# A two-layer transformer kernel: a gate ahead of ten maxima, the last output tile in halves, and the order of the first loads

## The chip, the cores and the metric

The kernel runs on one core of one Trainium2 chip. The metric is device time in microseconds (us) of one execution, as the median of several runs. The core has a matrix engine (PE, TensorE), VectorE (DVE), ScalarE (ACT), GpSimd (POOL) and SyncE (SP), which only issues transfers. Each engine works through a queue of its own in order; they meet at semaphores. Matrix products land in eight banks of PSUM of 128 partitions by 512 numbers.

## The reference

Two layers on x of shape (2, 512, 512), that is eight tiles of 128 rows, four to a batch b:

```python
xn = _layernorm(x)
x = x + attention0(xn)  # 32 heads of 16, 8 key-value heads, rope, causal softmax
      + ffn0(xn)        # 512 -> 1792 -> 512, silu gate, weights w * (su @ sv)
xn = _layernorm(x)
x = x + attention1(xn)  # 4 heads of 128, sigmoid of the scores, causal
      + ffn1(xn)        # 512 -> 1376 -> 512, silu gate, weights w + 2 * b @ a
```

## The kernel before, in words

All is 32-bit. A product of two 32-bit matrices is made of three faster ones: each operand is split into a high part (a rounded copy) and a low part (the difference), and `three_pass` (lines 50 to 54) issues high x high, low x high and high x low. So nearly every operand has a "hi" made by ACT and a "lo" made by a subtraction on POOL or DVE.

**Front (`qkv_stage`, lines 446 to 755).** SP loads the first four tiles of x (L497), then the key columns of the qkv weights (L498, 128 of 768 columns), then the rest of them (L500, four transfers), the other four tiles (L501) and tables. For each tile DVE takes mean and variance (L88, L90), ACT the root (L94), DVE the reciprocal (L98 or L636). Tiles 0 and 2 are normalised by DVE (L100), tiles 1 and 3 by ACT (L577), which needs a shift from DVE (L640). PE transposes the tile (L108), ACT makes the high part (L117) and DVE the low part (L122). POOL splits the key columns (L538 and L540), ACT and POOL the rest (L593 and L543; the last quarter by DVE, L658). Between the transpositions PE multiplies an identity with itself into a bank that nobody reads (L726), 2, 2, 3 and 5 times; before them it does the same with a tile of ones (L730). The products of keys and queries (`pair`, L706) then start, first `pair(0)`, the keys of batch 0, which waits for all four low parts and for POOL's split of the key columns.

**Attention and up (`attention_stage`, lines 850 to 1217).** The gate and up products of layer 0's feed-forward network and its attention are woven together by steps. There are 14 chunks `o` of 128 hidden columns, each of 16 steps `r` (step = 16 o + r): steps 0 to 3 are the gate of batch 0, 4 to 7 its up, 8 to 11 the gate of batch 1, 12 to 15 its up. A step is one three-pass product of 512 columns. ACT takes tanh of the gate (L277) at steps 4 and 12; DVE forms the gated value (L284, `dve_gate`) at r = 5 and 13 and the hidden value (L290) at r = 8 and at r = 0 of the next chunk. The product of chunk `o` on a bank waits until that bank's last value was read: `pe.wait_ge(self.u if k == 0 else self.h, 2 * o + b)` (line 804), `u` being counted by the gate and `h` by the hidden value.

Every third step, from step 6 on, ends with a burst of attention work. A group is four heads of one batch. In four bursts PE makes scores only to find each row's maximum (L1149, 11 pieces), which DVE reduces (L1095, 16 maxima, each followed by an accumulator read) in two halves; DVE negates each half (L1104), PE transposes the negated values (`minus_max`, L1156), ACT copies them into a row (L1028) and sends two row transfers to the stack of queries (L1038). The final scores (`key_scores`, L1167) need those rows. For group 0 the burst at step 6 has six maxima and the one at step 12 has ten, with both negations; the burst at step 15 has the transposition of the first-finished half, the one at step 18 that of the other. At step 13 POOL makes a low part of the network's factors (L141, `stack_lo`), 32x768, wanted by PE at step 18. SP loads the stack of a later group once the row of the current one has landed (L941, L942). Banks go round in two rings, `wide` and `narrow`, three banks each.

**End (`down1_stage`, lines 1909 to 1956).** The last down projection: for each batch, 11 chunks, each with four tiles' three-pass products over 512 columns (`pe_chunk`, line 385) into four banks that stay open over the chunks. ACT makes the high part of a hidden chunk (L377), POOL the low part (L382). When a tile's last chunk is done, DVE adds the bank to the running sum (L1949) and SP stores 256 KB (L1925).

The lines that are touched most:

```python
def dve_gate(self, dve, o, b):
    dve.wait_ge(self.tanh, 2 * o + b + 1)
    ...
if r in (5, 13):                      # attention_stage, vector, L1124
    up.dve_gate(dve, o, r // 8)
...
for t in range(NT):                   # down1_stage, vector, L1947
    dve.wait_ge(down.full, t + 1)
    dve.tensor_tensor(e.acc[:, t, :], e.acc[:, t, :], down.acc(t)[:, :], ALU.add).then_inc(out_s, 1)
```

## Time and profile before

| | us |
|---|---|
| median of three runs (661.47 to 661.97) | 661.49 |
| the profiled execution, its own time | 659.51 |
| its span, first to last instruction | 657.8 |
| PE busy | 647.8 (98%) |
| DVE busy | 413.1 (63%) |
| ACT busy | 287.9 (44%) |
| POOL busy | 244.4 (37%) |
| granted PE clock, mean | 0.999 |

The profile is one execution. Times in it count from the start of the span. Busy time of PE includes pipelining: a record of 0.39 us for a product of 512 columns overlaps its neighbours, and what counts is the distance between starts. "Idle before" names the work whose semaphore came last. A line number can be that of a helper.

### The profile page before, as it was taken

The page shows a single profiled execution, that of the slowest core. Times are in us where ns is not written, and L with a number is a line of the kernel's source. Part 1 is how long each engine was busy: PE and PEld are TensorE (multiplying, and loading weights), DVE is VectorE, ACT ScalarE, POOL GpSimd, SP SyncE. Part 2 cuts the span into 40 slices and gives each one's busy share as a digit, 9 for nine tenths or more (in the row PEclk, how much of TensorE's full clock was granted, in tenths as well). Part 3 has the DMA queues.
Part 4 walks back from the last instruction along what each step waited for, and adds up shares of the span by engine and source line. Part 5 has one row for each costly group of instructions (what it writes and reads, how often), then busy time and mean ns, then how long its engine had stood idle before and what let it go on. Part 6 is the DMA issues. An engine that isn't in the chain of part 4 may idle for free.

```text
span 657.8 us, 9974 instructions
## 1 busy us (share of the span) xinstructions
PE 647.8 (98%) x3472; PEld 495.5 (75%) x3472; DVE 413.1 (63%) x985; ACT 287.9 (44%) x559; POOL 244.4 (37%) x245
## 2 busy tenths in 40 slices
PE   7999999999999999999999999999999999999998
PEld 6887666666666666666788888888888888888886
DVE  6958777667777677663477665386665655646501
ACT  5333455455455555544344344264444444443321
POOL 4597333123323233323144538503234323323443
PEclk9999999999999999999999999999999999999999
DMA  9457323253323222021255600501011101012011
GB/s 303 138 158 183 96 80 111 80 134 95 90 57 90 79 79 80 18 81 50 74 184 163 211 21 17 147 1 33 32 33 35 62 33 33 32 34 79 15 50 65
DMA packets 23929, 55.17 MB, mean 84 GB/s; under 512 B 3876, under 2 KB 4872, under 8 KB 22824
## 3 DMA queue, kind: packets, MB, share of 16 engines
q1 hardware_dynamic: 23224, 54.35, 27.8%
q8 instruction: 28, 0.46, 0.3%
q10 hardware_dynamic: 656, 0.20, 0.1%
q14 instruction: 21, 0.17, 0.1%
HBM read 42.86 MB, written 11.54 MB: 83 GB/s over the span
## 4 chain that ended last, share of the span: by engine, by line
PE 97%; DVE 2%; DMA 0%; ACT 0%; issue 0%
PE bank L52 26%; PE bank L54 25%; PE bank L53 25%; PE bank L1149 7%; PE bank L1180 6%; PE bank L1167 2%; PE bank L180 2%; PE bank L108 1%; PE bank L1156 1%; PE bank L344 1%; PE bank L1744 1%; DMA x<-in_x 0%; DVE bank L1095 0%; DVE acc L1949 0%; PE bank L1505 0%; DVE minus_max L1104 0%
## 5 line engine op out<-in xcount | busy, mean ns | idle before, releaser
L1095 DVE CUSTOM_DVE_ANT_0 bank<-bank,mask 128x512 f32<-128x512 f32 (+3 forms) x256 | 118.1, 521 | 44.2 <-PE bank L1149 44.0
L217 POOL TENSOR_TENSOR up_w_lo<-up_w_eff,up_w_hi 128x512 fp32r<-128x512 f32 x50 | 66.9, 1346 | 103.0 <-ACT up_w_hi L213 103.0
L382 POOL TENSOR_TENSOR down_h_lo<-hidden,down_h_hi 128x512 fp32r<-128x512 f32 x50 | 65.1, 1304 | 89.0 <-ACT down_h_hi L377 89.0
L52 PE MATMUL bank<-x0T_hi,up_w_hi 128*128 128x512 f32 x224 | 94.7, 423 | 2.6 <-DVE up_gated L284 2.6
L1047 ACT ACTIVATE probs<-bank 128x512 f32<-128x512 f32 x160 | 84.5, 597 | 22.4 <-PE bank L1167 22.4
L54 PE MATMUL bank<-x0T_lo,up_w_hi 128*128 128x512 f32 x224 | 88.5, 395 | 0.0
L53 PE MATMUL bank<-x0T_hi,up_w_lo 128*128 128x512 f32 x224 | 88.4, 395 | 0.0
L52 PE MATMUL bank<-down_w_hi,down_h_hi 128*128 128x512 f32 x200 | 78.3, 391 | 0.0
L53 PE MATMUL bank<-down_w_hi,down_h_lo 128*128 128x512 f32 x200 | 78.0, 390 | 0.0
L999 POOL TENSOR_SCALAR_AFFINE_SELECT probs<-probs 128x512 f32<-128x512 f32 x64 | 39.9, 636 | 98.9 <-ACT probs L1047 98.9
L377 ACT ACTIVATE down_h_hi<-hidden 128x512 fp32r<-128x512 f32 x50 | 31.5, 631 | 89.6 <-PE bank L54 89.6
L284 DVE SCALAR_TENSOR_TENSOR up_gated<-up_tanh,bank 128x512 f32<-128x512 f32 x50 | 34.3, 685 | 42.3 <-ACT up_tanh L277 42.0
L52 PEld LDWEIGHTS bank<-x0T_hi,up_w_hi 128*128 128x128 f32 x224 | 42.1, 188 | 20.1 <-issue 14.1
L1149 PE MATMUL bank<-k_stack,q_stack 48*128 48x512 f32 (+3 forms) x256 | 56.9, 342 | 0.0
L1167 PE MATMUL bank<-q_stack,k_stack 49*128 49x512 f32 x160 | 54.0, 434 | 0.0
L213 ACT ACTIVATE up_w_hi<-up_w_eff 128x512 fp32r<-128x512 f32 x50 | 31.1, 630 | 51.2 <-DVE up_w_eff L204 51.2
L290 DVE SCALAR_TENSOR_TENSOR hidden<-up_gated,bank 128x512 f32<-128x512 f32 x50 | 34.2, 685 | 29.6 <-PE bank L54 29.3
L1149 PEld LDWEIGHTS bank<-k_stack,q_stack 48*128 48x128 f32 x256 | 35.9, 185 | 22.1 <-issue 17.1
L277 ACT ACTIVATE up_tanh<-bank 128x512 f32<-128x512 f32 x50 | 29.7, 594 | 46.5 <-PE bank L54 25.3
L54 PEld LDWEIGHTS bank<-x0T_lo,up_w_hi 128*128 128x128 f32 x224 | 42.1, 188 | 10.2
L53 PEld LDWEIGHTS bank<-x0T_hi,up_w_lo 128*128 128x128 f32 x224 | 42.3, 189 | 6.0
L1708 POOL TENSOR_SCALAR_AFFINE_SELECT weights_T<-weights_T 128x128 f32<-128x128 f32 x32 | 9.9, 310 | 93.5 <-ACT weights_T L1700 93.5
(173 smaller groups left out, 1387.8 us busy)
## 6 DMA issues: line engine op xcount, KB each, us to landing
w_raw<-in_w_gate_up SPq DMA_DIRECT2D x25, 512.0 KB, 3.5
w_raw<-in_w_down SPq DMA_DIRECT2D x25, 256.0 KB, 2.9
q_stack<-q_hi SPq DMA_DIRECT2D x32, 128.0 KB, 3.4
att<-att_T SPq DMA_DIRECT2D x16, 256.0 KB, 2.0
q_hi<-rope_hi SPq DMA_DIRECT2D x8, 256.0 KB
q_lo<-rope_lo SPq DMA_DIRECT2D x8, 256.0 KB
q_stack<-q_lo SPq DMA_DIRECT2D x16, 128.0 KB, 3.4
attention_or_xn<-att SPq DMA_DIRECT2D x16, 128.0 KB
```

The lines of the kernel that those rows point to most:

```text
L52: pe.matmul(out, w_hi, m_hi, start=first, stop=False, skip_group_check=True)
L53: pe.matmul(out, w_lo, m_hi, start=False, stop=False, skip_group_check=True)
L54: return pe.matmul(out, w_hi, m_lo, start=False, stop=last, skip_group_check=True)
L217: pool.tensor_tensor(self.half(self.w_lo[:, o % 2], k), self.half(self.w_eff, k), f32(self.half(self.w_hi[:, o % 2], k)), ALU.subtract).th ...
L284: dve.scalar_tensor_tensor(out=self.ut[:, b, :], in0=self.th[:, b, :], scalar=1.0, in1=self.product_bank(o, b, 0)[:, :], op0=ALU.add, op1= ...
L382: pool.tensor_tensor(self.h_lo[:, k % 2, :], self.hid[:, o, b * S:(b + 1) * S], f32(self.h_hi[:, k % 2, :]), ALU.subtract).then_inc(self.h ...
L999: pool.affine_select(out=diag, in_=diag, compare_op=ALU.is_ge, fill=0.0, base=0, pattern=[[0, REP], [1, P]], channel_multiplier=-1).then_i ...
L1047: act.activation(pt[:, BLOCK_OF[KEY_PIECES[p]], :, :], key_ring(g, p).bank(("keys", g, p))[:, :].rearrange("p (h s) -> p h s", h=REP), ACT ...
L1095: dve.tensor_tensor_reduce(out=own, in0=own, in1=e.mask[:, S - w:S], scale=1.0, scalar=NEG, op0=ALU.add, op1=ALU.max, accum_out=rmax[:, i ...
L1149: last = pe.matmul(bank[:, n * w:(n + 1) * w], qst[K, slot, h + n, i * P:(i + 1) * P], kst[K, slot, 0:w], start=(n == 0), stop=(n == nh - ...
L1167: pe.matmul(key_ring(g, p).bank(("keys", g, p))[:, :], kst[K, slot, j * P:(j + 1) * P], qst[K, slot, :, i * P:(i + 1) * P], start=True, st ...
L1180: last = pe.matmul(bank[32 * h:32 * (h + 1), j * P:], e.v[:, b, j, kv, :], pt[:, own, h, :], start=(j == 0), stop=(j == NJ - 1), skip_grou ...
```

## The change

Three parts. In the front, the key columns are loaded after the third tile of x and before the fourth; DVE normalises tile 3 itself, so that ACT normalises tile 1 only; the identity products become 4, 0, 0 and 9; and POOL begins the low parts of the other weight columns only after the four low parts of x. In the attention stage the gate of chunk 0, batch 1, goes ahead of the burst at step 12 (it stood at step 13); the first transposition of negated maxima follows step 14 instead of step 15; POOL's low part at step 13 waits for the first negation. At the end, the last low part is made by DVE instead of POOL; the last tile's chunks 0 to 8 are added early; its chunks 9 and 10 are left until the other three tiles are done, and are computed, added and stored in two halves of 256 columns in banks 3 and 4, the second half stored from ACT's queue.

```diff
@@ qkv_stage
-        shift = sb("norm_shift", [P, NJ])
+        shift = sb("norm_shift", [P, 1])
-        norm.normed_in_order = {0: (norm.normed, 1), 1: (act_normed, 1), 2: (norm.normed, 2), 3: (act_normed, 2),
-                                **{t: (norm.normed, t - 1) for t in range(NJ, NT)}}
+        norm.normed_in_order = {0: (norm.normed, 1), 1: (act_normed, 1), **{t: (norm.normed, t) for t in range(2, NT)}}
-        IDENTITY_PRODUCTS = (2, 2, 3, 5)
+        IDENTITY_PRODUCTS = (4, 0, 0, 9)
@@ qkv_stage, sync
             for t in range(NJ):
                 sp.dma_start(x_sb[:, t, :], d["x"][t * P:(t + 1) * P, :]).then_inc(x_loaded[t], 16)
-            sp.dma_start(w_raw[:, :, 0:P], d["w_qkv"][:, 0:P].rearrange("(c p) n -> p c n", p=P)).then_inc(w_loaded[0], 16)
+                if t == 2:
+                    sp.dma_start(w_raw[:, :, 0:P], d["w_qkv"][:, 0:P].rearrange("(c p) n -> p c n", p=P)).then_inc(w_loaded[0], 16)
@@ qkv_stage, gpsimd
+            pool.wait_ge(norm.lo, NJ)
             for c in range(NC - 1):
                 pool.wait_ge(w_hi_ready, c + 1)
@@ qkv_stage, scalar
             norm.act_hi(act, 1)
-            normalise(3)
             norm.act_hi(act, 2)
@@ qkv_stage, vector
             norm.dve_norm(dve, 2)
-            reciprocal(3)
-            shift_of(3)
+            norm.dve_norm(dve, 3)
@@ attention_stage
+FIRST_ROW_AT, EARLY_GATE_AT = 14, 12
@@ attention_stage, gpsimd
                     pool.wait_ge(*stage.last_pair_low)
+                    pool.wait_ge(neg_done, 1)
                     stack_lo(pool, e.lr0, e.lr0_raw, slice(0, 0), LR0_REST[part], e.lr0_hi, part + 2, e.lr0_lo)
@@ attention_stage, vector
-                if r in (5, 13):
+                if r in (5, 13) and step != EARLY_GATE_AT + 1:
                     up.dve_gate(dve, o, r // 8)
+                if step == EARLY_GATE_AT:
+                    up.dve_gate(dve, 0, 1)
@@ attention_stage, tensor
                     for half, g in ((0, s["low"]), (1, s["high"])):
-                        if g is not None:
+                        if g is not None and (g, half) != (0, 1):
                             minus_max(g, half)
+                if step == FIRST_ROW_AT:
+                    minus_max(0, 1)
@@ down1_stage
+        LAST = 2 * CH1 - 1
+        HALVES, last_banks = [slice(0, D // 2), slice(D // 2, D)], [e.bank[3], e.bank[4]]
+
+        def store_half(engine, half):
+            t, cols = NT - 1, HALVES[half]
+            engine.wait_ge(out_s, NT + half)
+            engine.dma_start(out[t * P:(t + 1) * P, cols], e.acc[:, t, cols]).then_inc(stored, 16)
...
-            for t in range(NT):
+            for t in range(NT - 1):
                 sp.wait_ge(out_s, t + 1)
                 sp.dma_start(out[t * P:(t + 1) * P, :], e.acc[:, t, :]).then_inc(stored, 16)
-            sp.wait_ge(stored, 16 * NT)
+            store_half(sp, 0)
+            sp.wait_ge(stored, 16 * (NT + 1))
@@ down1_stage, gpsimd
-                for o in range(2 if b == 0 else 0, CH1):
+                for o in range(2 if b == 0 else 0, CH1 - b):
@@ down1_stage, scalar
                 down.act_hhi(act, 1, o)
+            store_half(act, 1)
@@ down1_stage, vector
+            for t in range(NJ):
+                add(t)
+            dve.wait_ge(down.hlo, 2 * CH1 - 1)
+            dve.wait_ge(down.hhi, 2 * CH1)
+            dve.tensor_tensor(down.h_lo[:, LAST % 2, :], down.hid[:, CH1 - 1, S:], f32(down.h_hi[:, LAST % 2, :]),
+                              ALU.subtract).then_inc(down.hlo, 1)
+            t = NT - 1
+            dve.wait_ge(down.mm, 2 * CH1 - 3)
+            dve.tensor_tensor(e.acc[:, t, :], e.acc[:, t, :], down.acc(t)[:, :], ALU.add).then_inc(rest_added, 1)
+            for t in range(NJ, NT - 1):
+                add(t)
+            t = NT - 1
+            dve.wait_ge(rest_added, 1)
+            for half, cols in enumerate(HALVES):
+                dve.wait_ge(down.full, NT + half)
+                dve.tensor_tensor(e.acc[:, t, cols], e.acc[:, t, cols], last_banks[half][:, cols], ALU.add).then_inc(out_s, 1)
@@ down1_stage, tensor
-            for b in range(B):
-                for o in range(CH1):
-                    down.pe_chunk(pe, b, o)
+            for o in range(CH1):
+                down.pe_chunk(pe, 0, o)
+            for o in range(CH1 - 3):
+                down.pe_chunk(pe, 1, o)
...
+            pe.wait_ge(down.hlo, 2 * CH1 - 2)
+            for i in range(NJ):
+                last = product(CH1 - 3, i)
+            last.then_inc(down.mm, 1)
+            pe.wait_ge(down.hlo, 2 * CH1 - 1)
+            for i in range(NJ - 1):
+                product(CH1 - 2, i)
+            pe.wait_ge(down.hlo, 2 * CH1)
+            for i in range(NJ - 1):
+                product(CH1 - 1, i).then_inc(down.full, 1)
+            pe.wait_ge(out_s, 2)
+            for half in range(2):
+                last_product(half, CH1 - 2)
+                last_product(half, CH1 - 1).then_inc(down.full, 1)
```

`product(o, i)` is the three-pass product of chunk `o` for tile `4 + i` over 512 columns; `last_product(half, o)` is that of the last tile over the 256 columns of one half, into bank 3 or 4.

## Rows read from the trace of the kernel before

**Rows 1.** The page, part 4: the chain that ended last, shares by engine.
```profile
PE 97%; DVE 2%; DMA 0%; ACT 0%; issue 0%
```
**Rows 2.** Time line, PE, 63 to 68 (start us, us, engine, line, operation, count, idle before).
```profile
63.70 0.40 PE L52 MATMUL bank<-x0T_hi,up_w_hi 128*128 128x512 f32 x1
...
64.40 0.27 PE L1156 MATMUL bank<-ident,minus_max 128*8 128x128 f32 x1
67.31 0.47 PE L52 MATMUL bank<-x0T_hi,up_w_hi 128*128 128x512 f32 x1 [2.65 <-DVE up_gated L284]
```
**Rows 3.** Time line, 60 to 68, the other engines.
```profile
60.20 0.60 ACT L277 ACTIVATE up_tanh<-bank 128x512 f32<-128x512 f32 x1 [3.03 <-PE bank L54]
...
61.26 0.56 DVE L1095 CUSTOM_DVE_ANT_0 bank<-bank,mask 128x384 f32<-128x384 f32 x1 [1.53 <-PE bank L1149]
...
61.99 1.82 POOL L141 TENSOR_TENSOR lr<-lr_raw,lr 32x768 fp32r<-32x768 f32 x1
...
62.44 1.41 DVE L1104 TENSOR_SCALAR minus_max<-row_max 128x8 f32<-128x8 f32 x1
...
65.00 1.81 ACTq L1038 DMA_DIRECT2D q_stack<-minus_max_rows  x2
...
66.41 0.17 DVE L1104 TENSOR_SCALAR minus_max<-row_max 128x8 f32<-128x8 f32 x1
...
67.27 0.69 DVE L290 SCALAR_TENSOR_TENSOR hidden<-up_gated,bank 128x512 f32<-128x512 f32 x1
...
67.86 0.31 SPq L941 DMA_DIRECT2D q_stack<-q_hi  x1
```
**Rows 4.** Time line, 7 to 13, the front.
```profile
7.33 0.68 DVE L88 BATCH_NORM_STATS2 norm_stats<-x 128x6 f32<-128x512 f32 x1
...
8.31 0.55 DVE L100 TENSOR_SCALAR x<-x,norm_mv,norm_rstd 128x512 f32<-128x512 f32 x1
...
8.53 1.47 POOL L540 TENSOR_TENSOR wqkv_lo<-wqkv_raw,wqkv_hi 128x512 fp32r<-128x512 f32 x1
...
8.55 0.65 PE L108 MATMUL bank<-ident,x 128*128 128x128 f32 x4 [1.03 <-ACT x L577]
...
9.10 1.47 DVE L122 TENSOR_TENSOR x0T_lo<-bank,x0T_hi 128x512 fp32r<-128x512 f32 x2
...
11.08 1.28 PE L726 MATMUL bank<-ident 128*128 128x128 f32 x10
...
12.66 0.50 PE L52 MATMUL bank<-x0T_hi,wqkv_hi 128*128 128x512 f32 x1 [0.29 <-DVE x0T_lo L122]
```
**Rows 5.** Time line, 649 to 656, DVE and POOL.
```profile
649.93 1.29 POOL L382 TENSOR_TENSOR down_h_lo<-hidden,down_h_hi 128x512 fp32r<-128x512 f32 x1 [1.43 <-ACT down_h_hi L377]
...
652.56 2.73 DVE L1949 TENSOR_TENSOR acc<-acc,bank 128x512 f32<-128x512 f32 x4 [27.19 <-PE bank L54]
```
**Rows 6.** Issue of the key weights; transfers issued 2.4 to 2.9, KB, us to landing.
```profile
2.66 0.43 SPq L498 DMA_DIRECT2D wqkv_raw<-in_w_qkv  x1
...
x<-in_x SPq DMA_DIRECT2D x1, 256.0 KB, 4.7
wqkv_raw<-in_w_qkv SPq DMA_DIRECT2D x1, 256.0 KB, 5.1
```
**Rows 7.** Line L100, layer 1's normalisations: ns min/median/max, first and last start.
```profile
L100 DVE TENSOR_SCALAR attention_or_xn<-acc,norm_mv,norm_rstd x8: 545/546/1331, 389.7 to 433.5; 128x512 f32<-128x512 f32 x8
```
**Rows 8.** Time line, PE, 459 to 460: three products of 256 columns, then 512.
```profile
459.62 0.28 PE L52 MATMUL bank<-x1T_first,xk_hi 128*128 128x256 f32 x1
...
459.97 0.40 PE L52 MATMUL bank<-x1T_second,up_w_hi 128*128 128x512 f32 x1
```
**Rows 9.** Line L366, a subtraction of DVE in SBUF: ns min/median/max.
```profile
L366 DVE TENSOR_TENSOR down_w_lo<-down_w_eff,down_w_hi x14: 627/693/1361, 317.4 to 359.7; 128x512 fp32r<-128x512 f32 x14
```
**Rows 10.** The transfer issued between 655.2 and 655.5: KB, us to landing.
```profile
out<-acc SPq DMA_DIRECT2D x1, 256.0 KB, 2.0
```
**Rows 11.** Time line, PE, the first instructions.
```profile
1.81 3.61 PE L730 MATMUL bank<-v_ones 128*128 128x128 f32 x18 [1.81 <-POOL v_ones L536]
```

More of the change, by code:

```diff
@@ L575, in normalise @@
             def normalise(t):
-                act.wait_ge(shifted, 1 + t // 2)
-                act.activation(x_sb[:, t, :], x_sb[:, t, :], ACT.Identity, bias=shift[:, t:t + 1],
+                act.wait_ge(shifted, 1)
+                act.activation(x_sb[:, t, :], x_sb[:, t, :], ACT.Identity, bias=shift[:, :],
                                scale=norm.rstd[:, t:t + 1]).then_inc(act_normed, 1)
@@ L639, in shift_of @@
                 dve.wait_ge(norm.rst, t + 1)
-                dve.tensor_scalar(shift[:, t:t + 1], norm.mv[:, t, 0:1], norm.rstd[:, t:t + 1], -1.0,
+                dve.tensor_scalar(shift[:, :], norm.mv[:, t, 0:1], norm.rstd[:, t:t + 1], -1.0,
                                   ALU.mult, ALU.mult).then_inc(shifted, 1)
@@ L1917, in down1_stage @@
         layer1.up.down_factor_read = [(down.eff, 1), (down.eff, 2)]
-        out_s, stored = sem("out_ready"), sem("stored")
+        out_s, stored, rest_added = sem("out_ready"), sem("stored"), sem("last_tile_rest_added")
+        LAST = 2 * CH1 - 1
[4 more added lines that the diff above has]
+            engine.dma_start(out[t * P:(t + 1) * P, cols], e.acc[:, t, cols]).then_inc(stored, 16)
         def sync(sp):
@@ L1946, in vector, with add @@
             dve.wait_ge(*before["added"])
-            for t in range(NT):
+            def add(t):
                 dve.wait_ge(down.full, t + 1)
                 dve.tensor_tensor(e.acc[:, t, :], e.acc[:, t, :], down.acc(t)[:, :], ALU.add).then_inc(out_s, 1)
-        def tensor(pe):
-            for b in range(B):
-                for o in range(CH1):
-                    down.pe_chunk(pe, b, o)
+            for t in range(NJ):
+                add(t)
+            dve.wait_ge(down.hlo, 2 * CH1 - 1)
@@ new lines, in vector, with product, last_product @@
+            dve.wait_ge(rest_added, 1)
+            for half, cols in enumerate(HALVES):
+                dve.wait_ge(down.full, NT + half)
+                dve.tensor_tensor(e.acc[:, t, cols], e.acc[:, t, cols], last_banks[half][:, cols], ALU.add).then_inc(out_s, 1)
+        def tensor(pe):
+            for o in range(CH1):
+                down.pe_chunk(pe, 0, o)
+            for o in range(CH1 - 3):
+                down.pe_chunk(pe, 1, o)
+            def product(o, i):
+                k, own = CH1 + o, slice(i * P, (i + 1) * P)
+                return three_pass(pe, down.acc(NJ + i)[:, :], down.h_hi[:, k % 2, own], down.h_lo[:, k % 2, own],
+                                  down.high[o], down.low[o], False, o == (CH1 - 3 if i == NJ - 1 else CH1 - 1))
+            def last_product(half, o):
+                k, own, cols = CH1 + o, slice((NJ - 1) * P, S), HALVES[half]
+                return three_pass(pe, last_banks[half][:, cols], down.h_hi[:, k % 2, own], down.h_lo[:, k % 2, own],
+                                  down.high[o][:, cols], down.low[o][:, cols], o == CH1 - 2, o == CH1 - 1)
+            pe.wait_ge(down.hlo, 2 * CH1 - 2)
[12 more added lines that the diff above has]
+                last_product(half, CH1 - 1).then_inc(down.full, 1)
```

## The prediction, made before the result was known

> **What bounds the kernel now.** The page's chain comes first: TensorE (PE) carries 97% of it [rows 1]. So an edit counts only if it shortens PE's instruction stream, a hole in it, or one of its two ends. The time line of PE in the attention stage shows the one long hole inside: the products of step 15 begin at 63.70, the transposition of the negated maxima starts at 64.40, and the first product of step 16 waits until 67.31, 2.65 us idle, put down to the gate on VectorE (DVE) [rows 2]. The other engines' time line says why the gate is late: tanh is ready at 60.80 (60.20 + 0.60), but DVE runs ten maxima and two negations from 61.26 on, and only then the gate, which is done where the hidden row starts, near 67.2 [rows 3]. One negation of 128x8 took 1.41 us and its twin 0.17: the long one ended with the POOL subtraction L141 beside it (61.99 + 1.82 = 63.81) [rows 3]. Next the front: PE starts the key products at 12.66, after the fourth low part on DVE [rows 4]. Last the end: four additions 652.56 to 655.29, then the last store [rows 5].
>
> The sum is made against the profiled execution: span 657.8, its own time 659.51. The median of the three runs shown is 661.49, 1.98 above; I carry the same difference over to it.
>
> **Middle: the gate ahead of ten maxima.** The gate moves from step 13 to step 12 in DVE's queue. It waits for tanh at 60.80, runs 0.69 and ends near 61.52; DVE was idle until 61.26, so the maxima behind it start about 0.3 later. POOL's subtraction now waits for the first negation, so the 1.41 should become 0.17: 1.24 back. Maxima and both negations end near 66.58 (66.41 + 0.17) + 0.3 - 1.24 = 65.6, the hidden row at 66.4 instead of 67.96 [rows 3].
>
> What is PE's next wait? Step 16 needs the gate (61.5) and the low weights of chunk 1, long done; PE arrives at 64.66 and goes on. The new POOL wait holds L141 back to about 62.9 to 64.7; behind it stand only POOL's low weights, wanted only after step 18's factors, and PE's own wait for it at step 18, near 66.1. The moved transposition follows step 14 at 63.70 and finds its negation ready at 62.9. ScalarE copies the row near 64.0 instead of 64.71, and its two row transfers start 0.7 earlier. They took the ACT queue from 65.00 to 66.81, and SP, which waits for the second landing, went on at 67.86; both move to 67.16 at the latest [rows 3]. The first key scores, in step 18's burst, need the first of those rows and come at about 67.2 (64.66 + three steps of 0.70, as from 63.70 to 64.40, + some 0.4 for two factors and the first scores, from 0.23 for 512 columns): in time, by little [rows 2]. The hidden row of 66.4 is wanted at step 20, near 68.7. SP gains no DMA here and its stack loads go 0.7 earlier. The scores at step 12 issue as before; DVE has already given their banks back. So all 2.65 should go. Bounds: 0 to 2.65; I take 2.65, since each successor found has slack. If this cover were gone, the most that could return is the same 2.65.
>
> **Front.** The key weights are issued before the fourth tile of x. Their landings were 2.66 + 5.1 = 7.8, and 2.2 + 4.7 = 6.9 for the tile, whose issue stands about 0.45 before theirs [rows 6]. Swapped, the tile lands between 6.9 and 7.8 (nearest row: the keys, which held that place); I take 7.8. Its statistics were started by DVE at 7.33 and now start near 7.8: +0.45. Normalisation 2 followed them by 0.98 (7.33 to 8.31), so it runs from 8.8 to 9.3. In DVE's queue the small shift of tile 3 goes and a full normalisation of 0.55 comes, with its reciprocal: 9.4 to 9.95. The four low parts took from 9.10 to about 12.6, though two of them are 1.47, so some 0.6 of that was waiting; now they run one after another: 9.95 + 2 x 1.47 = 12.9 at most, 12.7 at 0.69 each [rows 4]. ScalarE loses its normalisation of tile 3, which isn't on this chain any longer. PE: after the fourth transposition, about 10.05 to 10.65, nine identity products instead of five. Ten instructions took 1.28, so a product (two instructions) is about 0.224 and nine are 2.0: end 12.65, the same moment. The key products therefore start near 12.7 against 12.66: 0.0 within a tenth. If the tile still lands at 6.9, both chains are 0.4 shorter: -0.35. If it lands 0.35 later than I say, +0.35. The four products after the first transposition (from about 7.1, 0.9 us) end near 8.0, and PE waits for ScalarE's normalisation of tile 1 until 8.55, so they are free; if that cover were gone, the two added ones would cost 0.45.
>
> A DVE operation that works on SBUF alone can stand still while POOL works: a normalisation took 1.33 us instead of 0.55 once [rows 7]. POOL's key subtraction (1.47, from 8.53, 0.7 after its weights landed) now starts near 7.6 and is over near 9.1; at worst it ends under normalisation 2, which would have ended at 9.3 anyway. POOL's rest of the weights now waits for the fourth low part, 12.7, when ScalarE has just made their first high part anyway; the second pair of products wants it three microseconds later. The queue of SP holds the same transfers with only this swap, so all behind it land as before.
>
> **End.** PE issues the same columns, but twelve products of 256 columns instead of six of 512. Three of 256 take 0.35 (459.62 to 459.97) [rows 8], so twelve take 1.40; three of 512 take 0.68, the pitch at which the four additions follow them (2.73), so six took 1.36: +0.04 at most, within the rounding. The last chunk now starts 0.68 earlier, after three tiles of the chunk before, at about 651.2. POOL's low part would be ready at 651.22 (649.93 + 1.29) [rows 5]; the change gives it to DVE, whose like took 0.63 to 0.69, and 1.36 beside POOL [rows 9]. POOL is done by then, so it is ready near 650.6; even 1.36 would cost only 0.1. The early addition for the last tile (0.69) and this subtraction lie in DVE's idle time ahead of 652.5. After PE's end there remains one addition of 256 columns instead of 0.69. It isn't in the trace; from 512 columns in 0.69 with some 0.15 fixed I estimate 0.42: -0.27. Then the last store: 256 KB landed 2.0 us after its issue [rows 10]. The four stores were issued 0.68 apart, so 256 KB go out in 0.68 or less, 128 KB in 0.34: a half store can be from 0 to 0.34 shorter, and up to 0.4 if it also stood behind its forerunners, which now start 0.7 earlier. The ACT queue issues it while SP is busy. I take 0.18 for the landing, midway: total -0.27 - 0.18 = -0.45, bounds -0.2 and -0.7.
>
> The Trainium skill, page "DMA: Bandwidth & Descriptors", section "Anatomy of one DMA", says that about 2 us of a DMA are fixed, whatever its size, mostly the receipt. By that rule halving the store saves nothing on its landing, and the end brings 0.25 instead of 0.45. The trace gives 2.0 us for 256 KB and has no store of 128 KB from here, so it leaves this open.
>
> **Sum:** -2.65 - 0.45 + 0.0 = -3.1. Profiled execution 656.4 (span 654.7), median 661.49 - 3.1 = 658.4. Bounds: front -0.35 and end -0.7 give 657.8; front +0.35, end -0.2 and a middle that loses 0.6 to a late row give 659.6.
>
> **Rivals.** (A) The front becomes the longer chain. The tile lands 0.4 later still, and POOL's key subtraction starts just ahead of a normalisation and holds it (1.33 instead of 0.55 [rows 7], +0.8): together with what stands above about +1.3, time 659.7. For it: the four low parts have no gap left on DVE. Against it: the key weights come earlier, which takes POOL out of the way.
>
> (B) The other side, slower than before: TensorE drops to its lower level, 1.2 GHz, ahead of the key products, since the identity products between the transpositions go from 2 and 3 to none. The very first products (18 instructions in 3.61, 0.20 each) are nearly twice as far apart as the identity products later (0.112) [rows 4, 11], though the page's clock line shows nothing below nine tenths. A product of 512 columns takes 0.23 at the upper level and would take 0.23 more at the lower; 14 of them eat the whole gain of 3.1, and twenty make 661.49 - 3.1 + 4.6 = 663.0. Against it: PE stood idle for 1.03 us before 8.55 [rows 4] and ran on at the full pace; after the change its gaps are shorter, and it is busy for 2 us right ahead of the key products.
>
> (C) The change doesn't do what it says: step 16 waits for several things, and if another than the gate held it until 67.31, only the end gains: 661.0. Against it: PE's first product starts 0.1 after the gate's end, and the low weights it also waits for stand in POOL's queue ahead of L141, which had started at 61.99 [rows 3].
>
> **How the numbers follow.** Forecast 0.80; A 0.08, 659.7; B 0.06, 663.0; C 0.06, 661.0. What a measurement of this kernel can tell from no change is about 0.2%, 1.3 us: the forecast and A are faster (0.88), C is the same (0.06), B slower (0.06). Range 657.4 to 660.0: the forecast's bounds, 0.4 for the spread from run to run, and A.
>
> **What would show it.** Right: no wait over 0.3 us on PE between 60 and 80; both negations at 0.17; L141 starting after the first; hidden row ending near 66.4. Key products starting at 12.3 to 13.1, the fourth low part and the ninth identity product ending together. The last addition near 0.42, and 2.4 us or less from PE's end to the last landing. Wrong: a key score, factor or product of step 16 to 20 idle for a microsecond; a normalisation over 1 us; granted clock under 1.00 before 20 us; or products of the first pair 0.4 apart.

## The result and the profile after

| | before | after |
|---|---|---|
| median of the runs, us | 661.48 (6 runs, 659.81 to 662.16) | 655.99 (6 runs, 655.61 to 657.34) |
| ratio after / before (under 1 is faster) | | 0.9924, 95% interval 0.991 to 0.9938 |
| profiled execution, its own time / span, us | 659.51 / 657.8 | 656.31 / 654.6 |
| TensorE busy, us | | 649.0 (99% of the span) |

The prediction for the profiled execution (656.4, span 654.7) came out within 0.1 us. The prediction for the median (658.4, range 657.4 to 660.0) was 2.4 us too slow: the median fell by 5.5 us, the profiled execution by 3.2. So the question of the experiments is where the other 2.3 us are. The agreement on the profiled execution is in part luck: the same kernel profiled again (h1 below) took 655.84, 0.5 less, and the middle came out 0.2 larger than its term while the front came out 0.1 dearer.

First what the trace of after shows of the steps. PE around step 16, in answer to [rows 2]:

```profile
63.82 0.27 PE L1159 MATMUL bank<-ident,minus_max 128*8 128x128 f32 x1
63.85 0.48 PE L52 MATMUL bank<-x0T_hi,up_w_hi 128*128 128x512 f32 x1
...
67.08 0.49 PE L1170 MATMUL bank<-q_stack,k_stack 49*128 49x512 f32 x1
```

The transposed negation stands at 63.82, before step 15's product at 63.85, and no row after it has an idle time in brackets up to the key scores at 67.08. The time line of the other engines in the same stretch, in answer to [rows 3]:

```profile
60.95 0.69 DVE L284 SCALAR_TENSOR_TENSOR up_gated<-up_tanh,bank 128x512 f32<-128x512 f32 x1 [1.09 <-ACT up_tanh L277]
61.56 0.56 DVE L1096 CUSTOM_DVE_ANT_0 bank<-bank,mask 128x384 f32<-128x384 f32 x1
...
62.73 0.17 DVE L1105 TENSOR_SCALAR minus_max<-row_max 128x8 f32<-128x8 f32 x1
...
63.03 1.84 POOL L141 TENSOR_TENSOR lr<-lr_raw,lr 32x768 fp32r<-32x768 f32 x1 [0.97 <-POOL down_h_lo L554]
...
64.43 1.81 ACTq L1039 DMA_DIRECT2D q_stack<-minus_max_rows  x2
...
65.46 0.17 DVE L1105 TENSOR_SCALAR minus_max<-row_max 128x8 f32<-128x8 f32 x1
65.55 0.69 DVE L290 SCALAR_TENSOR_TENSOR hidden<-up_gated,bank 128x512 f32<-128x512 f32 x1
...
67.29 0.31 SPq L941 DMA_DIRECT2D q_stack<-q_hi  x1
```

The gate runs ahead of the maxima, both negations take 0.17 (one was 1.41), POOL's subtraction starts behind the first, and the hidden row comes at 65.55 instead of 67.27. The two row transfers start at 64.43, 0.57 earlier, and the key scores of 67.08 did not wait for them; SP goes on at 67.29 instead of 67.86.

The front, in answer to [rows 4]:

```profile
7.67 0.69 DVE L88 BATCH_NORM_STATS2 norm_stats<-x 128x6 f32<-128x512 f32 x1 [0.28 <-DMA x<-in_x]
...
8.66 0.58 DVE L100 TENSOR_SCALAR x<-x,norm_mv,norm_rstd 128x512 f32<-128x512 f32 x1
...
9.35 0.55 DVE L100 TENSOR_SCALAR x<-x,norm_mv,norm_rstd 128x512 f32<-128x512 f32 x1
9.81 2.48 DVE L122 TENSOR_TENSOR x0T_lo<-bank,x0T_hi 128x512 fp32r<-128x512 f32 x4
```

and PE of the same stretch:

```profile
8.82 1.78 PE L108 MATMUL bank<-ident,x 128*128 128x128 f32 x12 [0.59 <-ACT x L578]
10.45 2.17 PE L725 MATMUL bank<-ident 128*128 128x128 f32 x18
12.37 0.48 PE L52 MATMUL bank<-x0T_hi,wqkv_hi 128*128 128x512 f32 x1
```

The fourth low part ends at 12.29 (9.81 + 2.48), and the key products follow the nine identity products without a wait at 12.37 (the row of these ends at 12.62, but ends on PE are modelled and overlap what comes next). So both chains end together, as the prediction had it for 12.65 to 12.7. The end, in answer to [rows 5, 10]:

```profile
649.16 2.05 DVE L1964 TENSOR_TENSOR acc<-acc,bank 128x512 f32<-128x512 f32 x3 [0.63 <-PE bank L54]
...
651.63 0.28 PE L54 MATMUL bank<-down_w_lo_last,down_h_hi 128*128 128x256 f32 x1
...
651.95 0.42 DVE L1982 TENSOR_TENSOR acc<-acc,bank 128x256 f32<-128x256 f32 x1 [0.23 <-PE bank L54]
652.40 0.36 ACTq L1930 DMA_DIRECT2D out<-acc  x1
```
```profile
out<-acc ACTq DMA_DIRECT2D x1, 128.0 KB, 1.8
```

The last addition takes 0.42. The half store lands 1.8 us after its issue (the 256 KB store of before: 2.0 [rows 10]), and the span ends 2.2 us after that issue at 652.40.

### The profile page after: what moved, and what is told of

The parts are those of the page before. It is cut to its first block, busy times and chain, and to the rows that moved or that the text cites. A ratio compares the mean times of both kernels' runs of the same rounds, so it can differ in the third digit from the quotient of the medians.

```text
span 654.6 us, 9995 instructions
## 1 busy us (share of the span) xinstructions
PE 649.0 (99%) x3480; PEld 497.1 (76%) x3480; DVE 413.8 (63%) x988; ACT 286.9 (44%) x558; POOL 242.6 (37%) x244
## 4 chain that ended last, share of the span: by engine, by line
PE 95%; DVE 2%; DMA 1%; SPq 1%; issue 0%
PE bank L52 26%; PE bank L54 25%; PE bank L53 25%; PE bank L1152 7%; PE bank L1183 6%; PE bank L1170 2%; PE bank L180 2%; DMA x<-in_x 1%; PE bank L1159 1%; PE bank L344 1%; DVE rope_products L675 1%; PE bank L1749 1%; PE bank L108 1%; DVE norm_stats L88 0%; DVE x0T_lo L122 0%; SPq L500 0%
## 5 line engine op out<-in xcount | busy, mean ns | idle before, releaser
L382 POOL TENSOR_TENSOR down_h_lo<-hidden,down_h_hi 128x512 fp32r<-128x512 f32 x49 | 63.8, 1304 | 87.7 <-ACT down_h_hi L377 87.7
L52 PE MATMUL bank<-down_w_hi,down_h_hi 128*128 128x512 f32 (+1 forms) x202 | 78.7, 390 | 0.0
L53 PE MATMUL bank<-down_w_hi,down_h_lo 128*128 128x512 f32 (+1 forms) x202 | 78.4, 388 | 0.0
L277 ACT ACTIVATE up_tanh<-bank 128x512 f32<-128x512 f32 x50 | 29.7, 594 | 46.5 <-PE bank L54 25.3
```

The costliest lines, as they stand in the source:

```text
L52: pe.matmul(out, w_hi, m_hi, start=first, stop=False, skip_group_check=True)
L53: pe.matmul(out, w_lo, m_hi, start=False, stop=False, skip_group_check=True)
L382: pool.tensor_tensor(self.h_lo[:, k % 2, :], self.hid[:, o, b * S:(b + 1) * S], f32(self.h_hi[:, k % 2, :]), ALU.subtract).then_inc(self.h ...
```

## The experiments

Two theories stand against each other, called K and D in what was put down before the runs f to h. **K**: the stall of 2.65 us costs more than itself, because TensorE drops to its lower level behind it, in most executions and not in the one whose profile was shown. **D**: the missing 2.3 us lie in the front, in the end, or in something that the middle edit frees later on. Each run is timed beside the kernel before on the same chip, whose median was 661.57, 661.86, 661.57 and 662.43 in the four groups of runs (e, f, g, h). Besides its time, each execution has a mean granted clock; that tells of executions that have no profile whether the clock fell in them. "Ratio" is the time of the run to that of before beside it.

**e1, the kernel before, unchanged,** for a second profile of it.

> The kernel before, unchanged, profiled once more, to see what a usual execution of it looks like beside the one first shown (span 657.8, at the low end of its six times of 659.8 to 662.2). Theory F (the gain beyond the forecast sits in the front): the span is 659 to 660 and the whole of the extra lies before 20 us, as products further apart or a later start of the key products than 12.66. Theory M (it sits in the middle): the wait of step 16 is longer than 2.65, about 4 to 5 us. Theory V (the kernel before merely varies by where its transfers fall): the extra is spread, or at another place each time. Ratio 1.000.

Measured: 661.53 (11 runs), ratio 0.9998, 95% 0.9988 to 1.0009; profiled execution 661.71, span 660.0. None of the three theories put down for it fits: the wait is the same 2.66 (M wanted 4 to 5), only 0.27 us lie ahead of 54 us (F wanted all of it), and most of the rest sits in one place (V wanted it spread). Its PE time line behind the stall:

```profile
67.59 0.76 PE L52 MATMUL bank<-x0T_hi,up_w_hi 128*128 128x512 f32 x1 [2.66 <-DVE up_gated L284]
68.16 0.63 PE L53 MATMUL bank<-x0T_hi,up_w_lo 128*128 128x512 f32 x1
68.58 0.63 PE L54 MATMUL bank<-x0T_lo,up_w_hi 128*128 128x512 f32 x1
...
70.72 0.49 PE L52 MATMUL bank<-x0T_hi,up_w_hi 128*128 128x512 f32 x1
71.04 0.39 PE L53 MATMUL bank<-x0T_hi,up_w_lo 128*128 128x512 f32 x1
```

The products behind the stall are 0.43 apart until 70.72 (the first 0.57) and 0.23 to 0.32 after it. The windows of the same profile (busy us of PE, PEld, DVE, ACT, POOL, then the granted clock, the DMA share and GB/s) say why:

```profile
64.00:67.00 3.00, 0.93 (x5) 0.43 (x3) 2.96 (x19) 0.27 (x1) 0.10 (x1) 1.00 0.00 1
67.00:68.00 1.00, 0.41 (x1) 0.44 (x2) 0.90 (x2) 0.00 (x0) 0.00 (x0) 0.75 0.01 2
68.00:69.00 1.00, 1.00 (x3) 0.72 (x3) 0.24 (x1) 0.00 (x0) 0.00 (x0) 0.50 0.00 0
69.00:70.00 1.00, 1.00 (x4) 0.80 (x3) 0.00 (x0) 0.00 (x0) 0.00 (x0) 0.50 0.60 170
70.00:71.00 1.00, 1.00 (x5) 0.90 (x4) 0.05 (x1) 0.00 (x0) 0.00 (x0) 0.55 0.88 191
71.00:72.00 1.00, 1.00 (x7) 0.48 (x5) 0.65 (x1) 0.32 (x1) 0.00 (x0) 1.00 1.02 143
```

The granted clock is 0.50, the level of 1.2 GHz, for some three microseconds right behind the idle time. The profile of before that the prediction was made from has the same stall and stays at full clock:

```profile
67.00:68.00 1.00, 0.69 (x3) 0.62 (x4) 0.85 (x2) 0.00 (x0) 0.00 (x0) 1.00 0.01 2
68.00:69.00 1.00, 1.00 (x7) 0.82 (x6) 0.00 (x0) 0.00 (x0) 0.00 (x0) 1.00 0.32 90
```

A time line's marks tell the parts apart, since the work between two equal instructions is the same in both kernels. Line L277 (tanh) has a row near 54, ahead of the stall, and the next but one near 73, behind it; L360 has its last row near 617. All three against the shown profile of before (53.96, 73.02, 617.12), and the time of the profiled execution against 659.51:

| profile | tanh at 54 (front) | tanh at 73 | last L360 | own time |
|---|---|---|---|---|
| e1, before again | +0.27 | +1.73 | +2.20 | +2.20 |
| e4, end only | +0.44 | +1.88 | +2.01 | +1.53 |
| e2, middle only | +0.33 | -2.55 | -2.52 | -2.52 |
| after | +0.14 | -2.74 | -2.72 | -3.20 |
| h1, after again | -0.33 | -3.21 | -3.19 | -3.67 |

From the first mark to the second e1 loses 1.46 and e4 loses 1.44: the price of the clock. In e4 it falls a microsecond after the products have begun again at 67.77 (0.85 in the window from 68, 0.50 from 69 to 72). Another 0.38 of e1 is lost between 356 and 437.

**e2, e3, e4, one part of the change each** in the kernel before: the middle (gate at step 12, transposition after step 14, POOL's wait), the front (order of loads, DVE's normalisation, identity products 4, 0, 0, 9, POOL's wait for the low parts of x), the end (last tile in halves). The edits in short:

```
 e2:  + if step == EARLY_GATE_AT: up.dve_gate(dve, 0, 1)
      + pool.wait_ge(neg_done, 1)
      + if step == FIRST_ROW_AT: minus_max(0, 1)
 e3:  + IDENTITY_PRODUCTS = (4, 0, 0, 9)
      + if t == 2: (load of the key weights)
      + norm.dve_norm(dve, 3)
      + pool.wait_ge(norm.lo, NJ)
 e4:  + for half in range(2): last_product(...), store_half(...)
```

> Only the attention part of the change: gate at step 12, first transposition after step 14, POOL's L141 behind the first negation. Forecast by the rows: -2.65 us, ratio 0.9960. Theory M: -4.5 to -5, ratio 0.993. Theory F: -2.65. No wait of PE at step 16, both negations 0.17.

> Only the front of the change: loads swapped, tile 3 normalised by DVE, identity products 4, 0, 0, 9. Forecast: 0.0, ratio 1.000, key products at 12.4 to 12.7. Theory F: -1.5 to -2.5, ratio 0.9965 to 0.9975, though the start of the key products moves by only 0.3. Theory M: ratio 1.000.

> Only the end of the change: last tile in halves, last low part by DVE. Forecast -0.45, ratio 0.9993; both theories the same, 0.999 to 1.000. If the end were the cause of the extra it would be under 0.997.

Measured: e2 657.12 (5 runs), ratio 0.9929 (0.9916 to 0.9941); e3 661.11 (11 runs), 0.9989 (0.9976 to 1.0002); e4 661.24 (11 runs), 0.9988 (0.9977 to 0.9998). The middle alone brings 4.4 of the 5.5 us, where its term was 2.65. So D is wrong for the front and the end: the extra gain belongs to the middle edit. In e3 and e4, as in e1, the stall is there, and 29 of their 33 executions have a mean clock of 0.997 (three microseconds at half clock in 660 are 0.0023). Of the 77 executions of before timed beside all these runs, 52 are at 0.997 or below. Eight of the other 25 lie under 660, where the shown execution lies. The mean clock sorts the 77 only roughly: the median is 660.87 for the 25 at 0.999 or 1.000, 661.74 for the 39 at 0.997, and 662.87 for the 13 lower. So by the medians a drop goes with 0.9 to 1.1 us, against 1.46 between the marks, and at full clock the shown execution is 1.4 faster than the middle.

**f1, f2, the stall filled.** Identity products into free columns and rows of the bank of the transposed negation, in the kernel before, right behind that transposition. The gate stays late and step 16 as late as before.

```
                         if g is not None:
                             minus_max(g, half)
+                        if (g, half) == (0, 1):
+                            for _ in range(10):        # f2: range(5)
+                                pe.matmul(row_ring(0, 1).bank(("minus_max", 0, 1))[64:P, P:2 * P],
+                                          e.ident[:, 64:P], e.ident[:, :], start=True, stop=True)
```

> The kernel before with ten products of the identity (64 output rows, 128 columns, two instructions each of 0.11 us, 2.24 us in all) put on TensorE right behind the transposed negation, inside the 2.65 us that step 16 waits; the gate stays late, so step 16 starts no earlier. Theory K (the wait also drops TensorE to 1.2 GHz for the 3 to 4 us behind it in most executions, worth about 1.9 us): the rest of the wait is 0.4 us, the granted clock stays at 1.00 behind it in 60 to 80, and the median falls by 1.5 to 2.0, to about 659.7. Rival D (the 1.9 us lie elsewhere: the clock rows are a by-product, or the late gate is still late further on): no change, 661.5.

> As the run before it, with five such products (1.12 us): the idle time ahead of step 16 is 1.5 us instead of 2.65, step 16 starts at the same moment. Theory K gives 659.7 if an idle time of 1.5 us is too short to drop the clock, 661.5 if not; I expect 659.7, since the kernel after shows 1.00 behind waits of 1 us. Rival D: 661.5.

Measured: f1 660.04 (10 runs), ratio 0.9975 (0.9964 to 0.9986); f2 660.29 (12 runs), 0.9981 (0.9969 to 0.9993). PE in f1:

```profile
65.18 2.40 PE L1210 MATMUL bank<-ident 128*64 128x128 f32 x20
67.91 0.47 PE L52 MATMUL bank<-x0T_hi,up_w_hi 128*128 128x512 f32 x1 [0.34 <-DVE up_gated L284]
```

and in f2:

```profile
64.89 1.31 PE L1210 MATMUL bank<-ident 128*64 128x128 f32 x10
67.63 0.47 PE L52 MATMUL bank<-x0T_hi,up_w_hi 128*128 128x512 f32 x1 [1.43 <-DVE up_gated L284]
```

Work that computes nothing, and that saves not a moment of the wait, makes the kernel 1.8 and 1.6 us faster than before beside it (intervals 0.9 to 2.4 and 0.5 to 2.1). From the tanh near 54 to the one near 73 both profiles take 19.07 us, as the shown profile of before (19.06), against 20.52 in e1. K holds and D falls. An idle time of 1.43 us was short enough in f2's profile, and by the mean clock in at least ten of its twelve executions.

**f3, f4, the middle edit taken apart.** f3 moves the gate only; f4 adds POOL's wait only.

```
 f3:  -  if r in (5, 13):                      f4:   pool.wait_ge(*stage.last_pair_low)
      +  if r in (5, 13) and step != 13:           + pool.wait_ge(neg_done, 1)
             up.dve_gate(dve, o, r // 8)
      +  if step == 12:
      +      up.dve_gate(dve, 0, 1)
```

> The kernel before with the gate moved from step 13 to step 12 and nothing else of the middle edit. Theory K: step 16 has no wait, so both parts are gained: 2.65 + 1.9 = 4.5, 657.0, though the long negation (1.41 us) remains; at most 0.3 more is lost on the transposition or the first row of the key scores. Rival E (the other parts of the middle edit are needed: the row of negated maxima comes late and takes the wait over): a wait of 0.7 to 1.5 us at the transposition of the negated maxima or at the key scores near 67, and 658.5 or more.

> The kernel before with POOL's subtraction held back behind the first negation and nothing else. The negation should take 0.17 us instead of 1.41, and the wait of step 16 shrink by 1.24 to 1.4 us. Theory K: 1.24 from the wait, plus 1.9 if the clock stays up after an idle time of 1.4 us: 658.4, or 660.3 if it falls all the same. Rival D: 660.3 in any case.

Measured: f3 657.65 (6 runs), ratio 0.9941 (0.9923 to 0.9958); f4 659.42 (7 runs), 0.9961 (0.9947 to 0.9975). Between the marks at 54 and 73 f3 gains 2.14 and f4 1.24, the whole middle edit 2.88. In f4 the stall is exactly 1.24 shorter (the rows below, DVE, POOL and PE). In f3 the negation still takes 1.26 us, and PE waits at the other transposition (last row).

```profile
63.11 0.17 DVE L1105 TENSOR_SCALAR minus_max<-row_max 128x8 f32<-128x8 f32 x1
...
63.42 1.84 POOL L141 TENSOR_TENSOR lr<-lr_raw,lr 32x768 fp32r<-32x768 f32 x1 [0.81 <-POOL down_h_lo L553]
...
66.75 0.47 PE L52 MATMUL bank<-x0T_hi,up_w_hi 128*128 128x512 f32 x1 [1.41 <-DVE up_gated L284]
```

and f3:

```profile
68.27 0.27 PE L1158 MATMUL bank<-ident,minus_max 128*8 128x128 f32 x1 [0.25 <-DVE up_w_eff L204]
```

That the negation's 1.24 us come from POOL's subtraction is shown: nothing else differs. f4's median falls by 2.4, the 1.24 and about as much again: the clock stays up once the stall is short. Rival E of f3 was wrong in size: the other parts of the middle edit are worth 0.7 us at the mark near 73 (2.88 - 2.14), and 0.5 at the last L360.

**g1, g2, a pause of the same length elsewhere,** in the kernel after. TensorE waits before the fifth chunk of the last down projection's second batch for operations of DVE on a tile nobody reads.

```
             for t in range(NJ): add(t)
+            dve.wait_ge(down.mm, CH1 + 3)
+            for n in range(3):                   # g2: range(2), and no fourth
+                dve.tensor_tensor(down.w_eff[:, :], down.w_eff[:, :], e.bank[3][:, :], ALU.add).then_inc(down.eff, 1)
+                dve.wait_ge(down.eff, CH1 + n + 1)
+            dve.tensor_tensor(down.w_eff[:, 0:256], down.w_eff[:, 0:256], e.bank[3][:, 0:256], ALU.add).then_inc(down.eff, 1)
...
             for o in range(CH1 - 3):
+                if o == 4: pe.wait_ge(down.eff, CH1 + 4)
                 down.pe_chunk(pe, 1, o)
```

> The kernel after with a pause put into TensorE far from the attention stage: before the fifth chunk of the second batch in the last down projection (near 630 us) it waits for four operations on VectorE that start when the fourth chunk ends (three of 128x512, 0.67 each, and one of 256 columns, 0.42), about 2.6 to 2.8 us idle. The kernel after is at 655.99 without it. Theory K (a pause of this length is followed by some 4 us at 1.2 GHz in most executions): 655.99 + 2.7 + 1.9 = 660.6, granted clock near 0.50 in the stretch behind it. Rival L (the drop belongs to the place in the attention stage, not to the pause): 655.99 + 2.7 = 658.7 and a clock of 1.00.

> The same with two operations (1.34 us): some 1.5 us idle at the same place. Theory K with what the kernels with a wait of 1.4 and 1.5 us showed in the attention stage (clock 1.00): 655.99 + 1.5 = 657.5. If a pause of this length drops the clock too: 659.4.

Measured: g1 660.42 (12 runs), ratio 0.998 (0.9968 to 0.9992); g2 658.5 (6 runs), 0.9949 (0.9931 to 0.9966). g1's profiled execution is one without the drop, and its pause is the length aimed at:

```profile
635.37 0.50 PE L52 MATMUL bank<-down_w_hi,down_h_hi 128*128 128x512 f32 x1 [2.68 <-DVE down_w_eff L1972]
```

But of its 12 executions eight have a mean clock of 0.997 and a median of 660.6, four have 1.000 and a median of 659.4; 655.9 + 2.7 = 658.6 would be the pause alone. In g2 none of six is below 0.999. So L, that the place matters, is wrong: by the mean clock the same idle time drops the clock far from the attention stage, between stretches of unbroken work, in two executions of three. That its windows would show 0.50 was not seen, since the execution profiled was not one of those. g2's median is 1.0 above what I expected, and not by the clock. Its profile has a wait of 1.32 us at 362.93 for POOL's low part L382, which the profile of after lacks; but the execution profiled is the slowest of the six (659.59), so this doesn't settle the median. The next section comes back to it.

**g3, g4, after without one of its parts.** g3 keeps the end of before, g4 the front of before (the hunks of e4 and e3 undone).

> The kernel after with the end of before (last tile in one piece): the edit of the end by itself, without the clock in the way. The prediction's term: 0.45 dearer than the kernel after, 656.4 (0.2 to 0.7: 656.2 to 656.7). The page of after suggests 0.4 to 0.8.

> The kernel after with the front of before (key weights behind the fourth tile). The prediction's term is 0.0, 656.0. The page of after shows the key products 0.29 earlier, of which 0.15 come back as a wait at 28.55, and TensorE at 60 us even 0.1 later than before; so between 655.8 and 656.3. A front that saved its whole 0.29 would give 656.3, one that costs 655.9.

Measured: g3 656.82 (6 runs), ratio 0.9924 (0.9907 to 0.994); g4 657.78 (6 runs, 656.43 to 659.99), 0.9937 (0.9914 to 0.9959). g3 is 0.8 above after's 655.99, just outside the 0.2 to 0.7 expected; the interval of the ratio is wider than the term. The end is better read from the marks: behind the last L360 the profiles of after, h1 and e4 gain 0.48, 0.48 and 0.48 (-3.20 + 2.72, -3.67 + 3.19, 1.53 - 2.01), e1 and e2 nothing. g4 was a surprise, by 1.5 us. Its profiled execution shows the drop in the front, from just ahead of 10 us to past 12, in the PE time line and in the windows (columns as for e1):

```profile
8.93 0.77 PE L108 MATMUL bank<-ident,x 128*128 128x128 f32 x4 [1.03 <-ACT x L577]
...
14.63 0.50 PE L52 MATMUL bank<-x0T_hi,wqkv_hi 128*128 128x512 f32 x1 [0.29 <-DVE x0T_lo L122]
```
```profile
8.00:10.00 2.00, 1.07 (x7) 1.07 (x8) 1.93 (x5) 1.23 (x5) 1.60 (x2) 0.83 1.02 395
10.00:11.00 1.00, 1.00 (x7) 1.00 (x7) 0.96 (x4) 1.00 (x2) 0.00 (x0) 0.50 1.00 381
11.00:12.00 1.00, 1.00 (x6) 1.00 (x6) 0.47 (x1) 0.68 (x2) 0.00 (x0) 0.50 1.03 387
12.00:13.00 1.00, 1.00 (x8) 1.00 (x7) 0.69 (x1) 0.04 (x1) 0.00 (x0) 0.63 1.04 397
```

That explains one of the six executions (658.82, mean clock 0.997). Two others are as slow at a mean clock of 1.000 (659.99 and 658.44), and no profile shows where.

**h1, h2, h3, the front taken apart:** h1 is after, unchanged; h2 is after with `IDENTITY_PRODUCTS = (2, 2, 3, 5)`; h3 is g4 with `IDENTITY_PRODUCTS = (4, 2, 3, 5)`.

> The kernel after, unchanged, beside the two that follow: 656.0, 655.6 to 657.4, and every execution with a mean granted clock of 0.999 or 1.000, since it has no idle time of TensorE over 0.6 us between its first identity product and the end.

> The kernel after with the identity products back at 2, 2, 3, 5 (12 instead of 13). Theory F (in the front too an idle TensorE now and then drops to 1.2 GHz; the two more products behind the first transposition keep it busy): the idle time ahead of the second transposition grows from 0.6 to about 1.0, some executions (about 1 in 8, as 9 of 66 of before with a clock of 0.994 or 0.995) show a clock of 0.997, median as after, 656.0. By my prediction's front term (VectorE's low parts set the key products' start as much as the identity products) the median is at 655.9 to 656.3 too; a theory by which TensorE alone sets it gives 655.5.

> The kernel after with the front of before, except that four identity products stand behind the first transposition instead of two. The one before it of this kind (two products) gave 657.78 with one execution of six at 0.997, whose profile showed the clock at 0.50 from 9 to 12.6 us behind an idle time of 1.03 us. Theory F: idle time 0.6, no execution at 0.997, 656.0 to 656.6. If the drop has nothing to do with that idle time: one execution in six or so at 0.997 all the same.

Measured: h1 655.9 (6 runs), ratio 0.9913 (0.9898 to 0.9928); h2 656.58 (5 runs), 0.9917 (0.9904 to 0.9931); h3 656.51 (6 runs, 656.07 to 659.38), 0.992 (0.9904 to 0.9936). The idle time ahead of the second transposition is 0.58 in h1 and h3 and 1.03 in h2, as expected, and the one execution of the 17 with a clock under 0.999 (0.997, 658.09) is h2's. But h2 shows that the identity products cost more than their count, in a way that neither expectation had:

```profile
9.09 0.66 PE L108 MATMUL bank<-ident,x 128*128 128x128 f32 x4 [1.03 <-ACT x L578]
...
10.47 0.83 PE L725 MATMUL bank<-ident 128*128 128x128 f32 x6
11.14 0.60 PE L108 MATMUL bank<-ident,x 128*128 128x128 f32 x4
...
13.15 0.50 PE L52 MATMUL bank<-x0T_hi,wqkv_hi 128*128 128x512 f32 x1 [0.30 <-DVE x0T_lo L122]
```

The products between the transpositions hold the last one back until 11.14 (in after all of them are over by 10.6, 8.82 + 1.78), and the last low part with it: key products at 13.15, against 12.35 in h1. At 54 us h2 is 0.84 later than h1 (+0.51 against -0.33), and its median 0.7 later.

h3's median is as expected, but its profiled execution took 659.38, 3.5 more than h1's, at a mean clock of 1.000. Its front is no slower than that of before (key products at 12.98); TensorE stands idle twice behind it:

```profile
21.33 0.50 PE L52 MATMUL bank<-x0T_hi,wqkv_hi 128*128 128x512 f32 x1 [1.08 <-DVE wqkv_lo L658]
...
31.61 0.50 PE L52 MATMUL bank<-x0T_hi,wqkv_hi 128*128 128x512 f32 x1 [1.25 <-DVE x0T_lo L122]
```
```profile
x<-in_x SPq DMA_DIRECT2D x1, 1024.0 KB, 12.1
```

The load of the second four tiles of x landed 12.1 us after its issue, against 8.3 in before; DVE waited 4.35 us for it, and what it does next came late. The tanh that stands near 54 elsewhere is at 57.16. So a load can cost more than a drop of the clock, and the mean clock doesn't show it.

## Why the prediction was right in its waits and wrong in its number

**The step that failed** is the middle term of the sum for the median: it stood at -2.65, "the most that could return is the same 2.65", and the clock behind the stall was put at nothing. Measured, the middle edit alone takes 4.4 us off the median (e2). The sentence "I carry the same difference over to it" hid the gap. The shown execution was 1.98 us faster than the median of before, and I took those 1.98 us for a constant of the measurement that after would have too. For the larger part they were the cost of what the change removes. e1 shows what the shown execution had not: 1.46 us of half clock behind the stall, 0.27 in the front, 0.38 between 356 and 437. By these profiles the stall of 2.65 us costs 2.9 us in some executions and 4.4 in most; by the medians sorted by clock the drop is worth 0.9 to 1.1. So 0.9 to 1.5 of the 1.98 are the clock. The rest is that the execution profiled was among the fastest of its kernel, which was chance. In after the profiled execution and the median are 0.3 apart.

**The middle** (predicted -2.65): -2.88 between the two marks in e2, after and h1 alike, and -4.4 in the median of e2. Every forecast of its chain came true within 0.3: the gate's end 61.64 (61.52), the hidden row's end 66.24 (66.4), both negations 0.17, PE's next wait none. f3 and f4 add that the gate alone would leave 0.5 to 0.7 of it, which the prediction didn't ask.

**The front** (0.0, bounds 0.35 either way): the key products start at 12.37 and 12.35, by 0.3 earlier than the 12.7 I gave; the nine products and the low parts end together, as told, and the tile's statistics start at 7.67. Two sizes were off: the four low parts follow each other at 0.62, not 0.69, and the identity products began at 10.45 and gave way at 12.37, not at 12.65. How much the front gains is less clear. Seven more profiles with the front of before and no drop there (e1, e2, e4, f1 to f4) start at 12.49 to 13.35, in the middle 12.93, six with the new front (after, e3, g1, g2, g3, h1) at 12.35 to 13.56, in the middle 12.57. Part of that spread is when the first tile of x lands: DVE starts its statistics between 3.79 and 4.37. Counted from there, the key products follow after 8.70 to 9.07 with the old front (before and those seven), and after 8.21, 8.43, 8.51, 8.65, 9.19 and 9.36 with the new one. So the new front brings up to 0.5 and costs 0.5 and 0.7 in two profiles of six. In e3 (9.36) the fourth tile, now behind the key weights, landed late: DVE waited 1.18 us for it, until 8.42, the lateness that rival A is made of. In g3 (9.19) TensorE's early products ran at about half their pace, though the granted clock reads 1.00 there (eight of these took 1.06 in after):

```profile
7.73 1.92 PE L725 MATMUL bank<-ident 128*128 128x128 f32 x8
```

In the middle the gain is 0.1 (counted from the first tile) to 0.4 (by the starts themselves), and six profiles with that spread don't set it apart from chance. The wait of 0.15 at 28.55 in after doesn't belong to the new front: e2 has one of 0.22 at 28.74 with the old one.

**The end** (-0.45): -0.48, and the last addition 0.42 as estimated. What the half store saves on its landing comes out near 0.2 (0.48 less the 0.27 of the shorter addition; 1.8 us to landing instead of 2.0). The prediction drew too much from the Trainium skill ("DMA: Bandwidth & Descriptors", section "Anatomy of one DMA"). That section, written for transfers that GpSimd issues, has a part that grows with the bytes beside the fixed 2 us; by its figure of 436 GB/s, 128 KB less would save an estimated 0.3, not nothing. The trace, with a store issued by ACT, agrees in kind: 0.2.

**The sum** for a usual execution, from the runs: 2.9 for stall and restart, 1.5 for the clock, some 0.4 front, 0.48 end: 5.3, against the 5.5 measured. With the lower figures for the clock (0.9) and the front (0.1) it is 4.4. So 0.2 to 1.1 us of the gain are not assigned to any part.

**The rivals.** A did not come in after: no normalisation was held, the longest took 0.58. The late tile that it starts from did come once, in e3. C is excluded by f3 and e2. B had the right mechanism, in the wrong kernel: I let the clock fall in the front of after, while it fell in before, behind the stall in most executions and, as the 13 mean clocks of 0.994 to 0.996 suggest, somewhere else too in some. Its evidence against, "PE stood idle for 1.03 us before 8.55 and ran on at the full pace", was true of that one execution, and g4's shows the contrary.

**What stays open.** Executions at full clock still differ by more than 3 us (656.07 to 659.38 in h3, 657.05 to 660.71 in f3, 659.46 to 662.80 in before). One place is the wait for POOL's L382 near 364: 1.32 in g2, 0.39 in g4, 0.16 in f4, none in before, after, e1. Others are the landings of the loads, as in h3 and e3, and the pace of the first products, as in g3. None was tried. Whether an idle time of 1.03 us in the front drops the clock is likely and not settled: of the kernels without the long stall, 7 executions of 51 with the old gap (e2, f1 to f4, g4, h2) are at 0.997, and none of 30 with a gap of 0.6 (after, g2, g3, h1, h3). Three of the seven are f2's and f4's, which also have a stall of 1.4 us.

## What to carry to other kernels

A stall of TensorE can have a second price behind it, and one profile doesn't show whether it is paid: compare the profiled execution's time and mean granted clock with the median of the runs before that execution is taken as typical, and ask of a difference between them whether the change would remove it. Here a wait of 2.65 us was worth 4.4, and ten idle-time products that compute nothing were worth 1.8. Filler products pay where TensorE would stand idle anyway and cost where they stand in front of a transposition that another engine waits for.

## What the runs showed of the hardware that I had not expected

- Behind an idle time of 2.65 to 2.68 us the granted clock was 0.50 for some three microseconds in most executions and 1.00 in others of the same kernel: a mean clock of 0.997 or less in 29 of 33 (e1, e3, e4), in 52 of 77 (before) and in 8 of 12 (g1). The fall itself is seen in the profiles of e1 and e4; before, e3 and g1 were profiled without it. Ahead of the wait TensorE had been busy without a break.
- Behind idle times of 1.41 and 1.43 us between full work the clock stayed at 1.00 (f4, f2), as behind 1.50 and 1.32 (g2) and 1.08 and 1.25 (h3); in g4's front it was 0.50 from 10 us on, after an idle time of 1.03 us that followed only transpositions and identity products, while the same 1.03 had no such fall behind it in before, e1, e2, e4, f1 to f4 and h2. The Trainium skill ("TensorE: Matmul & The Clock Gate", section "Part 1: The HAM clock gate") lets the clock depend on how busy the engine has been lately and says that the slow start of a kernel differs from run to run; these runs show the same in the middle of one, behind one and the same wait.
- The products cost 0.43 instead of 0.23 at the lower level, and the whole drop 1.46 us (e1) and 1.44 (e4).
- A negation of 128x8 on DVE took 1.26 to 1.41 us beside a subtraction of POOL and 0.17 without it, with nothing else changed (f4).
- A load of 1024 KB landed 12.1 us after its issue in one execution (h3) and 8.3 in another (before), with the same loads issued ahead of it.
